# Layer norm moments after the last reductions of a group, q and the transpose of x one slot earlier, maxima one slot later, in an attention and RWKV-style FFN block

## What is computed

```python
h = x @ W1 + b1                       # q, k, v of 16 heads of width 8
w = einsum('bhqd,bhkd->bhqk', q, k) / sqrt(8)
w = softmax(w * mask - (1 - mask) * 1e6)          # causal
a = einsum('bhqk,bhkd->bhqd', w, v) @ Wp + bp
x = layernorm(x + a)
xr = mu_r * x + (1 - mu_r) * x_prev;  xk = mu_k * x + (1 - mu_k) * x_prev
f = sigmoid(xr @ W_r) * (square(relu(xk @ W_k)) @ W_v)
out = layernorm(x + f)
```

## Time and profile before

| what | value |
| --- | --- |
| median of three runs | 695.85 us |
| the profiled execution | 695.07 us, its span 693.3 us |
| PE busy | 608.0 us, 88% |
| DVE busy | 546.5 us, 79% |
| ACT busy | 451.8 us, 65% |
| Pool busy | 416.0 us, 60% |
| mean granted PE clock | 0.939 |
| chain of waits | PE 65%, DVE 22%, ACT 4%, Pool 4% |

### The profile page before, as it was taken

How to read it: one execution, slowest core, us unless ns; L and a number is a source line. 1 busy time by engine, 2 the same in 40 slices (tenths; PEclk the granted TensorE clock), 3 DMA queues, 4 the chain that set the end, 5 groups by cost and what they waited for, 6 DMA issues and landing times.

```text
span 693.3 us, 17691 instructions
## 1 busy us (share of the span) xinstructions
PE 608.0 (88%) x6729; PEld 274.8 (40%) x6729; DVE 546.5 (79%) x1654; ACT 451.8 (65%) x871; POOL 416.0 (60%) x548
## 2 busy tenths in 40 slices
PE   4458899999999999999999999999999999898864
PEld 2123333444443434444443444444443434343433
DVE  1386778788898888888898988888888989883237
ACT  2103776777767677777777686777777676766821
POOL 4011425665758585766758494857667584858473
PEclk9555999999999999999999999999999999998966
DMA  4752535343544435453334435353544344301101
GB/s 131 136 139 47 153 66 150 70 130 62 136 80 83 120 79 154 79 155 79 127 69 121 107 63 141 78 153 81 144 81 128 70 110 101 58 7 29 32 17 30
DMA packets 72202, 65.80 MB, mean 95 GB/s; under 512 B 9333, under 2 KB 63926, under 8 KB 72118
## 3 DMA queue, kind: packets, MB, share of 16 engines
q1 hardware_dynamic: 71410, 64.41, 39.2%
q10 hardware_dynamic: 708, 0.26, 0.2%
HBM read 34.70 MB, written 29.88 MB: 93 GB/s over the span
## 4 chain that ended last, share of the span: by engine, by line
PE 65%; DVE 22%; ACT 4%; POOL 4%; issue 3%; DMA 1%; ACTq 1%; POOLq 0%; SPq 0%; DVEq 0%
PE ops L624 17%; PE sps L597 13%; DVE rowmax L843 12%; PE tps L559 10%; PE spare L482 9%; PE spare L502 5%; PE sps L582 5%; DVE attn L876 2%; ACT probs L765 2%; PE spare L534 2%; DVE stats L849 2%; DVE y L882 1%; PE spare L523 1%; PE spare L497 1%; POOL probs L1023 1%
## 5 line engine op out<-in xcount | busy, mean ns | idle before, releaser
L843 DVE TENSOR_REDUCE rowmax<-sps 128x1 f32<-128x512 f32 (+7 forms) x1024 | 401.3, 448 | 72.7 <-PE sps L597 70.9
L765 ACT ACTIVATE probs<-tps 128x512 f32<-128x512 f32 x640 | 347.3, 596 | 121.9 <-PE tps L559 121.8
L1023 POOL TENSOR_SCALAR_AFFINE_SELECT probs<-probs 128x512 f32<-128x512 f32 x256 | 158.5, 638 | 210.0 <-ACT probs L765 208.8
L624 PE MATMUL ops<-probs,vop 128*32 128x384 f32 (+3 forms) x2048 | 173.7, 446 | 6.1 <-POOL probs L1023 5.0
L559 PE MATMUL tps<-qop,kop 50*128 50x384 bf16 (+3 forms) x1024 | 127.0, 306 | 13.5 <-ACT probs L765 11.2
L597 PE MATMUL sps<-kop,qop 48*64 48x512 bf16 (+7 forms) x2048 | 129.9, 309 | 7.8 <-DMA kop<-d_parts 7.8
L582 PE MATMUL sps<-qmask,dup 64*128 64x128 bf16 (+1 forms) x640 | 69.9, 215 | 31.7 <-DVE rowmax L843 28.9
L624 PEld LDWEIGHTS ops<-probs,vop 128*32 128x32 f32 x2048 | 50.6, 109 | 89.7 <-issue 65.5
L559 PEld LDWEIGHTS tps<-qop,kop 50*128 50x128 bf16 x1024 | 34.3, 94 | 123.7 <-ACT probs L765 71.0
L582 PEld LDWEIGHTS sps<-qmask,dup 64*128 64x128 bf16 x640 | 31.3, 94 | 80.7 <-DVE rowmax L843 77.0
L597 PEld LDWEIGHTS sps<-kop,qop 48*64 48x64 bf16 x2048 | 43.0, 106 | 47.6 <-issue 18.2
(11 more groups left out here) (123 smaller groups left out, 572.5 us busy)
## 6 DMA issues: line engine op xcount, KB each, us to landing
qop<-d_parts SPq DMA_DIRECT2D x64, 192.0 KB, 4.5
kop<-d_parts SPq DMA_DIRECT2D x63, 192.0 KB, 5.2
d_parts<-qk_parts SPq DMA_DIRECT2D x15, 768.0 KB, 3.7
d_parts<-qk_parts SPq DMA_DIRECT2D x15, 512.0 KB, 4.7
d_parts<-qk_parts SPq DMA_DIRECT2D x17, 256.0 KB, 4.9
xa<-L_attn_x SPq DMA_DIRECT2D x16, 256.0 KB, 2.9
xres<-L_attn_x SPq DMA_DIRECT2D x16, 256.0 KB, 3.1
out<-result SPq DMA_DIRECT2D x15, 256.0 KB, 2.4
```

Source lines behind the costliest of these rows:

```text
L624: last = nc.tensor.matmul(ops[32 * t:32 * t + 32, BLK * a:SEQ], vop[:, par, a, QUARTET * half + t, hh, :], probs[:, g % 2, i, off:off + w] ...
L765: nc.scalar.activation(probs[:, g % 2, i, :], tps[:, bank(n), :], ACT.Exp, scale=SCALE)\
L843: last = nc.vector.reduce_max(rowmax[:, par, QUARTET * half + i, a:a + 1], sps[:, bank(n), off:off + w], axis=AX_X)
L1023: last = nc.gpsimd.affine_select(out=v, in_=v, compare_op=ALU.is_ge, fill=0.0, base=0, pattern=[[0, QUARTET], [1, BLK]], channel_multiplie ...
```

## The change

The two calls of `layer_norm_moments` in DVE's loop move from the middle of their group (between the reductions of chunks 1 and 2) to its end, behind the reductions of chunks 2 and 3 and the spare use of slot 1. In `SPARE_USES` q goes from slot 1 to slot 0 of group 0, and xT and max0 change places in group 6. Pool's search for the maxima now looks at both slots of the group before, so it splits max0 at the same place in its program, the head of group 7.

```diff
 SPARE_USES = {
-    ("X", "xT"): (6, 1),
-    ("A", "q"): (0, 1), ("A", "k"): (1, 1),
-    ("S", "v"): (9, 0), ("S", "max0"): (6, 0),
+    ("X", "xT"): (6, 0),
+    ("A", "q"): (0, 0), ("A", "k"): (1, 1),
+    ("S", "v"): (9, 0), ("S", "max0"): (6, 1),
...
-    return at // GROUPS, at % GROUPS, 0
+    return at // GROUPS, at % GROUPS
...
-                    if tg == 4 and active("D", tb) and before("D", tb) < LAST:
-                        n = before("D", tb)
-                        is_read(dve, "project", n)
-                        layer_norm_moments(y, 0, n, stats_done, moments_done)
...
-                    if tg == 9 and active("E", tb) and before("E", tb) < LAST - 1:
-                        n = before("E", tb)
-                        wait(dve, z_done, n + 1)
-                        layer_norm_moments(z, 1, n, stats2_done, moments2_done)
                     if active("S", b):
                         reduce_chunk(before("S", b), g, 2)
                         reduce_chunk(before("S", b), g, 3)
                     for _, use, n in ORDER[b, g, 1]:
                         spare_use(use, n)
+                    if tg == 4 and active("D", tb) and before("D", tb) < LAST:
+                        n = before("D", tb)
+                        is_read(dve, "project", n)
+                        layer_norm_moments(y, 0, n, stats_done, moments_done)
+                    if tg == 9 and active("E", tb) and before("E", tb) < LAST - 1:
+                        n = before("E", tb)
+                        wait(dve, z_done, n + 1)
+                        layer_norm_moments(z, 1, n, stats2_done, moments2_done)
...
-                        for _, due, n in ORDER.get(shifted(b, g, -1), []):
+                        for _, due, n in ORDER.get((*shifted(b, g, -1), 0), []) + ORDER.get((*shifted(b, g, -1), 1), []):
```

## The result

| | before | after |
|---|---|---|
| median, us (lowest to highest) | 695.65 (694.54 to 697.23) | 706.22 (701.18 to 708.88) |
| profiled execution, us (its span) | 695.07 (693.3) | 707.99 (706.2) |
| PE waits for the reductions, all S masks, us | 28.9 | 36.6 |
| length of an undisturbed middle step, us | 38.31 | 38.15 |

The changed kernel is slower: 1.0142 times the time before, interval 1.0076 to 1.0207, 4 executions of each (the fourth of before, 695.46 us, puts its median at 695.65 instead of 695.85). 691.5 us was forecast, and 706.22 is outside the range of 686 to 698. It is the case that the prediction called rival 2.

A forecast was written before the change was run, and what follows sets the result against it. PE bounds the kernel (busy 145.82 of 154 us), so only its holes can be won. q -4.2, groups 5 and 6 +0.65 and the end steps total -4.4: 690.7 for the profiled execution, 691.5 as median, range 686 to 698.

The forecast's parts named there:

- rival 2: PE wait of about 1.0 us before group 6's masks halves the clock; nine of thirteen steps give 703; chance 0.15.
- The price of a fall: PE behind the group 6 wait: about 1.3 us lost each time (0.83 on P·V, 0.2 on T, rest on S).
- Nine of thirteen steps: Clock falls after the group 6 wait in nine of thirteen steps: 691.5 + 11.7 = 703 us.
- The collision: Group 5: Pool's mask starts inside the normalises of result and blocks the last, 0.36 us on DVE, which PE waits for.
- Rival 1: Group 5: mask starts 0.1 later, behind the last normalise, so no collision; 686.9 us; chance 0.2.
- The moments of y: Groups 4 and 5: PE's 0.57 hole closes, 0.74 us gained and given back at later masks; alone worth 0.
- q in slot 0: Groups 0 and 1: q's rest done earlier, S products of group 1 at 329.14 instead of 329.46, 0.32 us won per step.
- Rival 3: Groups 9 to 1: DVE or Pool's mask of group 9 later by 0.3, q brings nothing; 695.7 us; chance 0.15 with other no-effect ways.
- xT and max0: Group 6 swap: xT fills PE's 0.23 hole in slot 0; uncovered, it would bring 0.23 to 0.30 us.
- The ends: Steps outside the middle: first T step -0.45, the one before -0.3, first layer norm step -0.5, last two +0.4 us.

The follow-up runs named there:

- the store: Kernel before plus one VectorE memset (128x512, unused buffer) ahead of the reduction of chunk 2 of group 5 in each of 13 steps; 704.33 us, 1.0095 times.
- the two with the start-up filled: Useless PE product ahead of each mask pair in the step where S runs without T: kernel before 687.22 us; changed kernel with y's moments put back 682.87 us.
- the Pool wait kernel: Changed kernel plus one wait: Pool's mask of group 5 waits until both halves of result are normalised; 692.09 us, 0.9936 times the time before.
- the kernel with the wait filled: Changed kernel plus one useless PE product (w1p by itself, 128x384) per step ahead of the masks of group 6; 696.31 us, 0.9997 times the time before.

## Why the prediction was wrong

**The step that failed** is the weighing of rival 2. The prediction had the mechanism, the place, the size of the wait (about 1.0; 1.04 and 1.03 measured), the eight P·V matmuls at half clock (1.94; its model, the row of 117.07, was 1.90 for sixteen of half the columns) and a time for it, 703. It gave this a chance of 0.15 and set against it that PE is full around a single hole. So its sum has no term for falls in the middle steps, and they took 13.1 us of the profiled execution. The window 312.7 to 319.5 shows PE full, 6.72 of 6.80 us, and at half clock. Full work behind the hole was no protection. The prediction had rows that spoke for a fall, the one at 117 after 0.57 and 0.46, and none that spoke against one after a wait of 1.0, since no middle step of the kernel before has such a wait. The absence of falls after 0.57 alone said nothing about 1.04. Nor is the fall at 117 as regular as one execution makes it look: that step has the waits of 0.57 and 0.46 in seven of the profiled kernels, and a fall behind them in three (before, q alone, the store; not in the moments of y put back, the swap alone and the two with the start-up filled). Half-clock stretches that come in some steps and not in others were to be expected. An unseen size, nearly twice what had been seen to be harmless, deserved an even chance; the prediction would then have been a range to 703 or above with "slower" as likely as "faster".

**The price of a fall** was mis-sized as well, at 1.3 us. Of a stretch of 3.4 us it is right (1.35 in the kernel after, 1.54 in the kernel with only the moments of y moved), but four of the five falls in the middle steps of the profiled execution last 6.8 us and cost 2.89 to 2.97. 1.3 was put together from P·V, T and S of 4 us and took no account of a longer stretch. Five falls then cost 13.1 and not 6.5. "Nine of thirteen steps" was too many and 1.3 too little, and 703 came out near 706 by these two errors.

**The collision** came as worked out. Mask 0.64, pair 0.94 instead of 0.60: +0.34 against the forecast +0.36, and 0.34 and 0.35 per step in the two comparisons that have it alone. The kernel in which Pool waits shows the cause: pair 0.60, and 0.34 gone. Rival 1, a mask 0.1 later, did not happen. By the spacing of the pairs (270.72 - 270.20 = 0.52 for two) the last normalise would begin at 270.98, and so it did, 0.03 behind the mask at 270.95; it took 0.69 instead of 0.34. At 117 the order was the other way, the normalise at 117.31 and the mask at 117.32, and it was again the normalise that lost (0.73), as at 119.41, 0.03 ahead of a mask, in the kernel with only the moments of y moved (0.74). The mask kept 0.64 each time. The rule of the Trainium skill's page "SBUF — State Buffer", section "SBUF: two separate sides", that the shared port pair is held for a whole instruction, is borne out by the 0.94 here as well: the last normalise ended 0.08 behind the mask. The same section gives the pair to whichever of the two starts first. By the starts on record at 117 and 119 the trace doesn't agree, for there the normalise was ahead by 0.02 to 0.03 and was the one blocked.

**The moments of y** alone, without the collision, are worth 0: shown by the Pool wait kernel, 37.81 with the moments moved and 37.81 with them in place. DVE's idle time ahead of the normalise is 0.48, where 308.87 - 308.45 = 0.42 was worked out.

**q in slot 0** was forecast at 0.32 per step and brought 0.31. S of group 1 followed after 3.78 us; 3.8 was said. Rival 3 fell.

**xT and max0** were forecast at 0.25 for the swap alone ("0.23 to 0.30") and brought 0.18. That is the one term a little small. Together with the collision 0.05 per step of net loss was expected; measured, 0.34 - 0.18 = 0.16. So the undisturbed middle step is 38.15, where 38.31 - 0.32 + 0.05 = 38.04 was forecast: 0.11 us in each of ten steps, 1.1 us.

**The ends** were counted and roughly. The first step with a layer norm was forecast to gain 0.5 by the moments of y, beside what q brings; it gained 1.47, but in another way. 38.66 - 37.77 = 0.89 is the fall at 117.2, which is absent (37.77 is this step in the kernel before with its start filled, which has no fall there); 37.77 - 37.26 = 0.51 is q and xT (37.26 with the moments of y put back); only 37.26 - 37.19 = 0.07 is the moments of y. The second step gained 0.98, of which 37.75 - 37.21 = 0.54 is by the moments of y: it has no `result` to normalise yet (the first is at 185.8), so no collision, and the closed hole of group 5 counts. The prediction put that 0.5 one step too early.

**What stays open.** Five of ten middle steps fall, with the same wait to 0.01 us (1.04 at 272.32, 1.03 at 310.46). Nothing found in the trace marks those that do; the stretches of half clock in the kernel after begin 41.0 us apart (312.7, 353.7, 394.6 and 510.7, 551.7, 592.6), one in each of three steps on end; behind the first three come two steps without. That the wait is the cause, though, rests on four kernels: two with one wait of 1.03 or 1.04 have five and six falls in ten steps, one with 0.69 and one with 0.19 have none. Every one of the eleven falls, and that of the kernel with the store, begins 1.7 to 2.6 us after the end of its wait. How long a single wait may be isn't shown: between 0.69 and 1.03 there are only the 0.79 with its one fall and the 0.71 of the first step, beside 0.38 and 0.24, with a fall in one kernel of three. The fall at the end of the kernel with the wait filled, 10.2 us at 632, wasn't looked into; all kernels have falls in their last 120 us, behind the middle steps, of 3.4 to 13.7 us.

## What to carry to other kernels

A reordering that leaves the sum of TensorE's waits nearly alike (1.77 and 1.94 us in a middle step here) can still lose, if it gathers them: two waits of 0.57 and 0.23 did nothing here; with one of 1.04 the kernel takes 706.22 us and without it 689.61, and 13 us of this, in the profiled execution, are TensorE's clock. When a working-out leaves one engine waiting longer in one place than anywhere in the trace of before, that size is unknown ground and needs a chance of its own, as large as the forecast's; the cheap test is a product that nobody reads in that hole, which took the falls away without making a step longer. And before moving work on VectorE, look what GpSimd does at the new time: here a mask that came 0.7 us earlier lengthened a pair of normalises from 0.60 to 0.94.

## What the runs showed of the hardware

One product of 128x256 ahead of each pair of masks, in the one step where PE mostly waits, raised the clock of the start-up from 0.50 to 1.00 (by the durations of its matmuls: 0.41 instead of 0.64 for S) and saved 8.7 us of the 696 (687.22 us; 682.87 with the rest). The Trainium skill's page "TensorE: Matmul & The Clock Gate", section "A second HAM failure mode: psum-queue depth-cycling", tells of a kernel whose short idle times between groups of matmuls sent the clock down and up again; here single waits of 1.03 and 1.04 us in an engine that is busy 453 of 480 us did so.

The clock record doesn't always tell of the start: in the profile of the kernel with the Pool wait it shows 1.00 for 24 to 60 us, while its S products take the 0.64 us that they take at 0.50 before. Its first entry is at 70.9 us. So for the start the durations of matmuls decide here, and not the record.
